# A bit-by-bit requantization on Trainium2: one of two lanes taken from ScalarE to VectorE

## The reference, cut to what matters

```python
def _act_quant(x):                      # QB = 127
    scale = QB / jnp.maximum(jnp.max(jnp.abs(x), axis=-1, keepdims=True), EPS)
    q = jnp.clip(jnp.round(x * scale), -QB - 1, QB) / scale
    return x + jax.lax.stop_gradient(q - x)

def _bitlinear(x, w):
    return jnp.einsum('bsd,od->bso', _act_quant(x), _weight_quant(w))

gv = _bitlinear(h, w_gv)                # 2048 x 2048 by 2048 x 16384, per core
value, gate = jnp.split(gv, 2, axis=-1)
u = value * jax.nn.silu(gate)           # 2048 tokens x 8192
out = _bitlinear(u, w_out)              # 8192 -> 2048
return residual + out
```

## Time and profile before

| | us |
|---|---|
| median of 2 runs | 7483.42 (7458.97 and 7507.86) |
| the profiled execution, its own time | 7456.67 |
| its span on the slowest core (7) | 7455.1 |
| spans of the 8 cores | 7432.3 to 7455.1 |

### The profile page before, as it was taken

How to read it: one execution, slowest core, us unless ns; L and a number is a source line. 1 busy time by engine, 2 the same in 40 slices (tenths; PEclk the granted TensorE clock), 3 DMA queues, 4 the chain that set the end, 5 groups by cost and what they waited for, 6 DMA issues and landing times.

```text
span 7455.1 us, 49097 instructions; the slowest of 8 cores (7432.3 to 7455.1 us)
## 1 busy us (share of the span) xinstructions
PE 3241.4 (43%) x13138; PEld 1322.7 (18%) x13138; DVE 4177.8 (56%) x3305; ACT 3081.1 (41%) x2970; POOL 350.1 (5%) x663
## 2 busy tenths in 40 slices
PE   2200202111057787777777775000650705335086
PEld 0000000000023333333333332000220202112032
DVE  3845384756654444444444445677776577576712
ACT  2520212121234444444444442565665465456511
POOL 2011000000000000000000000000000000000000
PEclk8555555555578888888888887555875857677587
DMA  8998301000033333333333331112434415234333
GB/s 185 315 330 265 96 0 45 23 23 20 23 104 125 126 118 123 116 127 122 120 116 126 127 116 62 57 62 65 147 119 132 132 55 175 94 107 136 110 125 112
DMA packets 217459, 853.69 MB, mean 115 GB/s; under 512 B 34656, under 2 KB 34656, under 8 KB 159840
## 3 DMA queue, kind: packets, MB, share of 16 engines
q1 hardware_dynamic: 83376, 436.26, 17.4%
q0 software_dynamic: 78512, 313.60, 13.6%
q10 hardware_dynamic: 55296, 100.69, 4.0%
HBM read 694.24 MB, written 167.77 MB: 116 GB/s over the span
## 4 chain that ended last, share of the span: by engine, by line
DVE 50%; ACT 20%; DMA 12%; issue 7%; PE 6%; POOL 2%; ACTq 2%; DVEq 1%; POOLq 0%; SPq 0%
DVE zt L80 17%; DMA ub<-u_sp 5%; DVE res L80 3%; ACT wqt L80 3%; ACT wqs L80 3%; DVE paby L80 3%; DMA wmean<-wgvt 3%; PE pout L1364 3%; DVE sg_t L80 2%; DVE u_r L80 2%; DVE gc_t L80 2%; DVE Mx L80 2%; ACT gc_t L80 2%; ACT sg_t L80 2%; DVE qwv L80 2%
## 5 line engine op out<-in xcount | busy, mean ns | idle before, releaser
L1364 PE MATMUL pout<-q_r,qo_r 128*128 128x512 bf16 x4096 | 911.3, 385 | 1117.2 <-DMA qo_r<-qo_sp 585.3
L1090 PE MATMUL pvg<-q,qwv 128*128 128x512 bf16 x4096 | 1057.0, 417 | 720.7 <-DVE u_r L80 559.8
L80 DVE SCALAR_TENSOR_TENSOR zt<-mq,zt 128x1024 f32<-128x1024 f32 x896 | 1098.5, 1226 | 160.8 <-DVE zt L80 157.7
L80 ACT ACTIVATE mq<-zt,pbh 128x1024 f32<-128x1024 f32 x896 | 1028.7, 1148 | 229.9 <-DVE zt L80 225.4
L1095 PE MATMUL pvg<-q,qwg 128*128 128x512 bf16 x4096 | 925.8, 379 | 0.0
L80 ACT ACT_TABLE_LOAD x81 | 103.9, 1283 | 1662.3 <-DVE q L80 404.3
L1364 PEld LDWEIGHTS pout<-q_r,qo_r 128*128 128x128 bf16 x4096 | 403.5, 99 | 1629.3 <-issue 1168.1
L1090 PEld LDWEIGHTS pvg<-q,qwv 128*128 128x128 bf16 x4096 | 426.9, 105 | 1320.4 <-issue 927.6
L1095 PEld LDWEIGHTS pvg<-q,qwg 128*128 128x128 bf16 x4096 | 400.8, 98 | 483.3
L80 DVE TENSOR_TENSOR ub<-ub,s2b 128x1024 f32<-128x1024 f32 x128 | 156.9, 1226 | 431.0 <-DMA ub<-u_sp 430.3
L80 ACT ACTIVATE sg_t<-gc_t 128x512 f32<-128x512 f32 x256 | 161.1, 629 | 553.9 <-DVE gc_t L80 553.9
(11 more groups left out here) (149 smaller groups left out, 3633.3 us busy)
## 6 DMA issues: line engine op xcount, KB each, us to landing
wld<-wgvt SPq DMA_DIRECT2D x128, 1024.0 KB, 4.9
qo_r<-qo_sp SPq DMA_DIRECT2D x128, 1024.0 KB, 5.7
wmean<-wgvt SPq DMA_DIRECT2D x64, 1024.0 KB, 7.7
wmean<-wgvt POOLq DMA_DIRECT2D x64, 1024.0 KB, 11.6
wo_r<-woutT POOLq DMA_DIRECT2D x128, 512.0 KB, 5.0
u_sp<-u_r POOLq DMA_DIRECT2D x64, 1024.0 KB, 4.9
ub<-u_sp POOLq DMA_DIRECT2D x256, 256.0 KB, 5.4
wmean<-woutT SPq DMA_DIRECT2D x64, 512.0 KB, 13.1
```

The source lines that it names most:

```text
L80: r = f(*a, **kw)
L1090: t.matmul(pvg[:, 2 * q * TS:(2 * q + 1) * TS], qwv[:, r * 2048 + k * 128:r * 2048 + (k + 1) * 128], q1[:, (ts * DC + k) * TS:(ts * DC + k ...
L1364: last = t.matmul(pout[:, d * TS:(d + 1) * TS], qo_r[:, base + d * 128:base + (d + 1) * 128], rhs, start=(j == 0), stop=(j == HC - 1))
```

## The change

Only `emit_q2_slice` and the one count that follows from it (`dg1_gate`) change. Lane 0 keeps its way: Sign on ScalarE, scalar_tensor_tensor on VectorE. Lane 1 is now done by VectorE alone, with two instructions per bit: a tensor_scalar, (z >= threshold) x 2^(7-k), into lane 1's columns of `mq2`, and a tensor_tensor that subtracts it from z. This form subtracts a power or nothing, where lane 0's adds or subtracts half of it; so the thresholds are shifted (2^(7-k) - 128.5) and lane 1's last copy has a bias of -128.0 instead of -0.5. Per pair VectorE then has 28 instructions instead of 20 and ScalarE 10 instead of 18.

```diff
-            vfin[(ts, u)] = vb + 20 * pp + 19 + lane
+            vfin[(ts, u)] = vb + 28 * pp + 27 + lane
...
+            E0, E1 = 0, 2 * TS
+            O0, O1 = 2 * TS, 4 * TS
...
                 for k in range(8):
-                    for lane in range(2):
-                        c0, c1 = lane * 2 * TS, (lane + 1) * 2 * TS
-                        v.wait_ge(sA.h, ab + 18 * p + soff(p) + 2 * k + lane + 1)
-                        v.scalar_tensor_tensor(
-                            out=zt2[:, c0:c1],
-                            in0=mq2[:, c0:c1], scalar=HYB_S[k],
-                            in1=(ub2 if k == 0 else zt2)[:, c0:c1],
-                            op0=ALU.mult, op1=ALU.add)
+                    v.wait_ge(sA.h, ab + 10 * p + soff(p) + k + 1)
+                    v.scalar_tensor_tensor(
+                        out=zt2[:, E0:E1],
+                        in0=mq2[:, E0:E1], scalar=HYB_S[k],
+                        in1=(ub2 if k == 0 else zt2)[:, E0:E1],
+                        op0=ALU.mult, op1=ALU.add)
+                    v.tensor_scalar(out=mq2[:, O0:O1],
+                                    in0=(ub2 if k == 0 else zt2)[:, O0:O1],
+                                    scalar1=float(2.0 ** (7 - k)) - 128.5,
+                                    scalar2=-2.0 * HYB_S[k],
+                                    op0=ALU.is_ge, op1=ALU.mult)
+                    v.tensor_tensor(out=zt2[:, O0:O1],
+                                    in0=(ub2 if k == 0 else zt2)[:, O0:O1],
+                                    in1=mq2[:, O0:O1], op=ALU.subtract)
...
-                    for lane in range(2):
-                        c0, c1 = lane * 2 * TS, (lane + 1) * 2 * TS
-                        sc.wait_ge(sV.h, vb + 20 * p
-                                   + (1 + lane if k == 0 else 2 * k + 1 + lane))
-                        sc.activation(out=mq2[:, c0:c1],
-                                      in_=(ub2 if k == 0 else zt2)[:, c0:c1],
-                                      func=AF.Sign, bias=pbh[:])
+                    sc.wait_ge(sV.h, vb + 28 * p + (1 if k == 0 else 3 * k))
+                    sc.activation(out=mq2[:, 0:2 * TS],
+                                  in_=(ub2 if k == 0 else zt2)[:, 0:2 * TS],
+                                  func=AF.Sign, bias=pbh[:])
...
-                                  in_=mq2[:, c0:c1], func=AF.Copy, bias=-0.5)
+                                  in_=mq2[:, c0:c1], func=AF.Copy,
+                                  bias=(-0.5 if lane == 0 else -128.0))
...
-        dg1_gate = sA.n + (18 * (NP // 2) + 8 if ts + 1 < NTS else 8)
+        dg1_gate = sA.n + (10 * (NP // 2) + 8 if ts + 1 < NTS else 8)
```

More of the change, by code:

```diff
@@ L1278, in _ @@
                         in1=ub2[:, c0:c1], op0=ALU.mult, op1=ALU.add)
-        assert sV.n == vb + 20 * NP
+        assert sV.n == vb + 28 * NP
         @SCA
@@ L1306, in _ @@
                         in_=q2c[:, lane * 1024:(lane + 1) * 1024]))
-        assert sA.n == ab + 18 * NP + (8 if mid_cb is not None else 0)
+        assert sA.n == ab + 10 * NP + (8 if mid_cb is not None else 0)
     prev_next_ok = None
```

## The result

The changed kernel takes 7856.13 us (median of 11 runs, 7836.12 to 7881.94); the kernel before, run beside it, 7467.97 (10 runs). The ratio is 1.0515, with a 95% interval of 1.0493 to 1.0537: slower by 5.2%. The forecast was 7840 us, in a range from 7780 to 7905. The profiled execution took 7836.12 us, with a span of 7834.6 on core 0, 379.5 us more than that of before.

What follows compares the result with a forecast made beforehand. VectorE's instruction list in four consecutive requantization slices was taken to set the time. 7456.7 us plus 375 for steps and 2 for stalls gives 7834, with a little for the run median 7840 us, range 7780 to 7905.

Steps and rivals of the forecast that it cites:

- What bounds the kernel: Four requantization slices of about 550 us, one behind the other, set the time; TensorE is late nowhere.
- The step: Per bit of a lane pair, VectorE takes 3.532 us instead of 2.800; over 512 steps, +375 us.
- The bounds 0.574 and 0.753: Lowest and highest length in us for lane 1's new TENSOR_SCALAR, worth -60 and +31 us around the sum.
- Rival A: Lane 1's TENSOR_SCALAR runs at one element per cycle, 1.226 us long: 8107 us in all; chance 4%.
- The gaps: Between VectorE's instructions in the slices: 0.174 us when waiting for two semaphores, 0.107 when waiting for one.
- ScalarE's saved work is worth nothing: In the slices, 512 Signs of 1.15 us disappear, 589 us of work beside the path, gaining no time.
- Loads at a pair's end: VectorE's 430.3 us of waiting for `ub` stay, 6.7 us a pair, since both loads keep their places.
- The sum: Profiled 7456.7 us plus 375 for the slices' steps and 2 for rare stalls gives 7834, taken as 7840 us.
- B: The gap of `zt` shrinks to 0.107 us because ScalarE is done early: 34 us less, 7800 us; chance 3%.
- D: Not slower: at pair boundaries loads land while VectorE works, all 430.3 us of waiting gone: 7404 us; chance 2%.
- C: The new TENSOR_SCALAR holds up GpSimd's issue of `ub` loads once a pair: 44 us more, 7878 us; chance 4%.
- One of the signs: TensorE's 150.55 us wait for ScalarE's mid-slice eviction must grow by about 47 us, or the prediction is wrong.

Runs made afterwards that it cites:

- experiment 1: The changed kernel with lane 1's TENSOR_SCALAR left out and its subtraction kept: 7440.34 us, ratio 0.9929 to the kernel before.
- 2: The changed kernel with lane 1's TENSOR_SCALAR issued twice: 8248.92 us, ratio 1.1042 to the kernel before.
- Experiment 4: The changed kernel with an additional, long-fulfilled wait for ScalarE ahead of each of lane 1's TENSOR_SCALARs: 7889.33 us, ratio 1.0545 to the kernel before.
- experiment 3: The kernel before with lane 1's Signs left out on ScalarE, VectorE's instructions keeping both waits: 7470.43 us, ratio 0.9996.
- 9: The kernel before with four `ub` tiles instead of two, so loads are issued a pair ahead: 7147.36 us, ratio 0.9599.
- 10: The changed kernel with four `ub` tiles instead of two, so loads are issued a pair ahead: 7505.52 us, ratio 1.005 to the kernel before.
- 5: The changed kernel with one more TENSOR_SCALAR of 128x2048 behind each pair's last instruction: 7849.03 us, ratio 1.0555 to the kernel before.
- 7: The changed kernel with three more TENSOR_SCALARs of 128x2048 behind each pair's last instruction: 7842.06 us, ratio 1.0516 to the kernel before.
- 8: The changed kernel with three more TENSOR_TENSORs of 128x1024 behind each pair's last instruction: 7832.49 us, ratio 1.0506 to the kernel before.

## Why the prediction was right, point by point

*What bounds the kernel.* Right. The slices follow each other on the path and TensorE hides none of their growth: it started on the first product after 648 us of waiting instead of 555, and experiments 1 and 2 move the whole time by what they move in a step.

*The step.* Forecast 3.532 us, measured 3.53. Its unmeasured term, the TENSOR_SCALAR, was taken at 0.692 us from a longer one with immediates and a slope from two with pointer scalars; it is 0.694. The bounds 0.574 and 0.753 were not needed. Rival A (1.226 us) is excluded by the row. The table row of the Trainium skill (VectorE: DVE Perf Modes, "The TRN2 errata") gave an estimate of 0.594 us; the trace disagrees with it by the same 0.1 us as it did for the TENSOR_TENSOR. What the prediction did not say is that the same section calls this row too low and measures a fixed part of about 150 cycles in place of 58. By that an estimate is (512 + 150) / 0.96 = 690 ns, which the 694 ns of the trace bear out.

*The gaps.* Right: 0.17 us with two waits, 0.11 with one, whatever the second one is waiting for. Experiment 4 shows it by changing nothing else, and experiment 1 turns it into a kernel 0.7% faster than the kernel before, most of it by this.

*ScalarE's saved work is worth nothing.* Right, and shown by itself in experiment 3.

*Loads at a pair's end.* Right to 8 us: 422.7 instead of 430.3. Experiments 9 and 10 show that the cost of the change does not depend on them.

*The sum.* Right in size, and nearer than it deserved. The forecast put 375 us on the steps and 2 on stalls. The slices' time grew by 369.9 us, a little less, because VectorE's waits for ScalarE became 6 us shorter (31.6 and 25.9), which the sum held at nothing; its waits for `ub`, the first load aside, are 403 us in both kernels by the median of the cores. Between the two spans are 379.5 us, but 11.6 of them lie ahead of the slices, where nothing was changed (the first multiplication is at 4690.29 after and 4678.68 before), and some 4 in the last product. That 377 stands so near to 379.5 is luck. The medians of the runs are 388 us apart (7856.13 - 7467.97); of the 18 beyond the slices the profiles show no cause, and the forecast of 7840 is 16 us low.

*The rivals.* A, B and D did not come: B and A are excluded by rows, D by the wait for `ub`, which shrank by 8 us and not by 430. C did not come here, but its mechanism is real: in experiments 5 and 7 it costs 16 and 23 us.

*What was off.* One of the signs was badly put: the prediction said that TensorE's wait of 150.55 us should grow by about 47, and that it is wrong otherwise. On the core of the profile the wait grew by 30, because TensorE itself ran at a granted clock of 0.84 instead of 0.99 in the half before it; the interval from start to start grew by 46. On the six cores whose clock was not lower the wait is 198.9 to 200.4 us, about 47 to 50 more. So the mechanism holds. A wait is what is left between two engines' times, and the interval is what should have been forecast.

## What to carry to other kernels

Balancing two engines by moving work from the one with more idle time to the one that is waited for lengthens the path, however the busy shares over the whole span look; read in the stage which engine's previous instruction is the last releaser. Where an engine's own list sets the pace, count instructions times (length plus gap), and count the semaphores that each waits for: here a second wait cost 0.07 us 512 times. Where something outside the change varies, as the last product does from core to core here, compare the stage that was changed, on all cores. And before shuffling the steps of such a list between engines, ask whether they are needed: one TENSOR_SCALAR did the work of eight steps and took 16% off the kernel.

## What the runs showed of the hardware that I had not expected

- A wait for a second semaphore costs VectorE about 0.07 us in the gap even if it was fulfilled more than a microsecond before (0.18 against 0.11 us over 448 instructions).
- A TENSOR_SCALAR of 128x2048 f32 lengthens GpSimd's DMA issues that begin during it (1.45 us for two instead of 1.06; with three in a row 2.25), less than by its whole length of 1.23 us each; a TENSOR_TENSOR of the same length does not. Once in each of the 64 pairs, it cost the slices 16 us, and 23 with three in a row.
- TensorE's granted clock in the last product, behind the same epilogue, differs between the cores of one execution: in 9 it was 0.81 on core 5 and 0.99 on core 0, 136 us against 112 for the same 512 matmuls. In 4, 8, 9 and 10 those that took 129 us and more are always both cores of a neighbouring pair (0 and 1, 4 and 5, 2 to 5, 6 and 7); in the profiles of the kernels before and after there are none.
